# FFN products of a transformer block in scaled fp16 parts, with the raw W1/W3 tile scaled on ScalarE

## The reference

```python
xn = layernorm(x)                               # no gain, no bias
q, k, v = heads(xn @ Wq.T), heads(xn @ Wk.T), heads(xn @ Wv.T)
attn = softmax(causal(q @ k.T / sqrt(32)))
s = merge(attn @ v) @ Wo.T
hidden = silu(xn @ W1.T) * (xn @ W3.T)          # [2, 1024, 2048]
g = silu(fwht(hidden) @ W2.T)                   # Walsh-Hadamard transform over 2048
out = x + s * g
```

## Time and profile before

| | before |
|---|---|
| time, median of 3 runs | 972.14 us (972.06 to 972.33) |
| the profiled execution: its time | 972.55 us |
| the profiled execution: its span | 970.8 us |
| TensorE busy (matmuls) | 959.4 us, 99% |
| VectorE busy | 707.1 us, 73% |
| ScalarE busy | 565.7 us, 58% |
| GpSimd busy | 357.2 us, 37% |
| DMA | 110.58 MB, mean 114 GB/s |

### The profile page before, as it was taken

One profiled execution on the slowest core, in us unless ns is written; L12 is line 12 of the kernel. 1 busy time (PEld: TensorE's weight loads), 2 busy tenths in 40 slices (PEclk: granted clock), 3 DMA queues, 4 the chain that ended last, 5 costly groups with the idle time before them and its releaser, 6 DMA issues. The chain is left out here.

```text
span 970.8 us, 18488 instructions
## 1 busy us (share of the span) xinstructions
PE 959.4 (99%) x6392; PEld 797.7 (82%) x6392; DVE 707.1 (73%) x1441; ACT 565.7 (58%) x1172; POOL 357.2 (37%) x587
## 2 busy tenths in 40 slices
PE   8999999999999999999999999999999999999997
PEld 7888888888888887888888888888888888878886
DVE  7777888888888887755554578888888888833343
ACT  4324777777777786623334166777777777832221
POOL 1896764656656442000001024453443543500000
PEclk9999999999999999999999999999999999999999
DMA  9793235232232405951145523233223232181111
GB/s 285 259 271 110 77 89 142 78 88 56 77 89 56 121 23 201 345 203 44 45 174 204 174 55 88 57 78 89 55 78 88 56 78 56 45 342 49 43 44 44
DMA packets 55757, 110.58 MB, mean 114 GB/s; under 512 B 5360, under 2 KB 22384, under 8 KB 55152
## 3 DMA queue, kind: packets, MB, share of 16 engines
q1 hardware_dynamic: 55664, 109.40, 37.1%
HBM read 75.56 MB, written 33.55 MB: 112 GB/s over the span
## 5 line engine op out<-in xcount | busy, mean ns | idle before, releaser
L1024 DVE TENSOR_TENSOR p_lo<-stage,p_hi 128x512 f16<-128x512 f32 (+2 forms) x288 | 188.3, 654 | 58.4 <-ACT p_hi L743 58.0
L1337 PE MATMUL f<-xt_hi,w_hi 128*128 128x512 f32 x512 | 202.0, 394 | 0.0
L1337 PE MATMUL f<-xt_hi,w_lo 128*128 128x512 f32 x512 | 201.8, 394 | 0.0
L1337 PE MATMUL f<-xt_lo,w_hi 128*128 128x512 f32 x512 | 201.5, 394 | 0.0
L733 ACT ACTIVATE stage<-s 128x512 f32<-128x512 f32 (+2 forms) x288 | 150.8, 524 | 82.9 <-PE s L1298 81.1
L743 ACT ACTIVATE p_hi<-stage 128x512 f16<-128x512 f32 (+2 forms) x288 | 158.8, 551 | 24.9 <-POOL stage L595 20.2
L1298 PE MATMUL s<-qk_st 98*128 98x512 f32 (+2 forms) x384 | 141.4, 369 | 0.0
L1011 DVE CUSTOM_DVE_ANT_0 m<-m,causal 128x1024 f32<-128x1024 f32 (+3 forms) x128 | 131.0, 1023 | 2.7 <-PE m L1282 2.7
L602 POOL TENSOR_TENSOR w_lo<-w,w_hi 128x256 fp32r<-128x256 f32 x128 | 118.3, 953 | 28.5 <-ACT w_hi L764 27.2
L595 POOL TENSOR_SCALAR_AFFINE_SELECT stage<-stage 128x128 f32<-128x128 f32 x192 | 57.4, 306 | 179.0 <-ACT stage L733 178.2
L1337 PEld LDWEIGHTS f<-xt_lo,w_hi 128*128 128x128 f32 x512 | 96.6, 189 | 18.2
(11 more groups left out here) (179 smaller groups left out, 1831.3 us busy)
## 6 DMA issues: line engine op xcount, KB each, us to landing
qk_st<-qk_parts SPq DMA_DIRECT2D x96, 256.0 KB, 4.3
w<-w1w SPq DMA_DIRECT2D x32, 512.0 KB, 3.6
qk_parts<-qk_hi SPq DMA_DIRECT2D x32, 256.0 KB, 3.2
qk_parts<-qk_lo SPq DMA_DIRECT2D x32, 256.0 KB, 4.3
wht_in<-w SPq DMA_DIRECT2D x4, 1024.0 KB, 10.9
w_butterflied<-wht_in SPq DMA_DIRECT2D x4, 1024.0 KB, 5.9
w_transformed<-g_hi SPq DMA_DIRECT2D x8, 512.0 KB, 3.2
w_transformed<-g_lo SPq DMA_DIRECT2D x8, 512.0 KB, 4.7
```

The source lines that it names most:

```text
L1024: dve.tensor_tensor(p_lo[s][:], expd[q % NE][:, 0:end - need], p_hi[s][:], ALU.subtract).then_inc(p_lo_done, 1)
L1337: mm = pe.matmul(F[m][:, 0, :], w, v, start=k == 0, stop=k == GMM - 1)
```

## The change

The FFN's up-projections use fp16 parts in place of fp32r parts, three matmuls for a product as before.

- x: a second pair of transposed tiles, x16_hi and x16_lo, is made from the same PSUM bank, times 2048 (X_TOP): one operation on ScalarE and one on VectorE for each of the 8 tiles of a batch, after the groups in X16_AFTER. A bank is given to the next transpose, to `bound_of_v` and to `transpose_v_scale` only when x16_lo of its tile is done. xt_hi and xt_lo stay, for q, k and v.
- W1/W3: in the first batch each of the 16 tiles gets a power of two from its sum of squares. ScalarE squares the tile (`w13_squares`, with a sum for each partition), TensorE adds over partitions with a matmul of ones in the last columns of bank X (`sum_of_squares`), VectorE makes the power, the scale and the factors that undo it, in five small operations (`scale_of_w13`). This is done for tile 0, for tiles 1 to 3, and for four groups of three. Tile 0 is squared in w13; SP loads tiles 1 to 15 once more for it (`scan_w13`, into stage, wv_raw and a new buffer scan). In heads 0 to 11 the Square stands in slot 5.
- In both batches ScalarE multiplies the raw tile by its scale, in place, in two operations of 128x512 (`scale_w13`) in slot 1, before `w13_high` in slot 2. The first tile of a batch is scaled and split after V tile 1 and no longer after group 8.
- tanh takes its scale from w13_half, and `hide` multiplies by w13_unscale.
- TensorE's order: in a slot with a context one of the slot's FFN matmuls is kept back until behind the context (`kept`).
- Buffers are laid out anew: p_hi and p_lo share their room with xt_hi and xt_lo; x16_hi and x16_lo are new.

The diff, cut to its core (layout, semaphores and the waits for the last columns of bank X are left out):

```diff
@@ -40,6 +40,8 @@
+ONES_AFTER = [3, 4, 5]
+X_TOP = 2048.0
 W2_SCALE = 0.5 * float(HID) ** -0.5
@@ -63,7 +65,7 @@
 COPY_AT = [8, 4]
-W13_AT = 2
+SQUARES_AT, W13_AT = 5, 2
 WO_AT = [1, 2, 7, 9]
@@ -77,6 +79,12 @@
 XT_AFTER = {4: (4,), 5: (5,), 6: (6, 7)}
+X16_AFTER = {2: (0,), 3: (1,), 4: (2, 3), 7: (6, 7), 8: (4,), 9: (5,)}
+X16_ORDER = [t for g in sorted(X16_AFTER) for t in X16_AFTER[g]]
+SCAN_AFTER = {10: (1,), 13: (2, 3)}
+SQUARES_AFTER = {8: (0,), 13: (1,)}
+SQUARES_OF_V = {4: (2,), 5: (3,)}
+SCAN_FIRST, SCAN_GROUP = 4, 3
 SPLIT_WK_AFTER, ROOT_AFTER = 1, 2
@@ -458,6 +517,8 @@
                         load_stack(sp, n + 2)
+                        if b == 0 and j + SCAN_FIRST < NH:
+                            scan_w13(j + SCAN_FIRST)
                         load_w13(n + 2)
@@ -599,7 +660,8 @@
                 at = (slice(None), piece // 2, slice(piece % 2 * (D // 2), (piece % 2 + 1) * (D // 2)))
-                pool.tensor_tensor(w13_lo[n % 2][at], w13[at], w13_hi[n % 2][at].bitcast(F32), ALU.subtract
+                pool.wait_ge(w13_scaled, 2 * n + piece // 2 + 1)
+                pool.tensor_tensor(w13_lo[n % 2][at], w13[at], w13_hi[n % 2][at], ALU.subtract
                                    ).then_inc(w13_lo_done, 1)
@@ -684,6 +747,11 @@
+
+            def x16(b, t):
+                act.wait_ge(xt_lo_done, b * NT + t + 1)
+                act.activation(x16_hi[:, :, t * P:(t + 1) * P], xt_bank(t).rearrange("p (k c) -> p k c", k=KT),
+                               ACT.Copy, scale=X_TOP).then_inc(x16_hi_done, 1)
@@ -712,8 +780,11 @@
                             split_wv(b, kt)
-                    if g == 2 * KT:
-                        w13_high(b * NH)
+                    for t in X16_AFTER.get(g, ()):
+                        x16(b, t)
+                    if b == 0:
+                        for t in SQUARES_AFTER.get(g, ()):
+                            w13_squares(t)
                 if b == 0:
@@ -722,8 +793,23 @@
                                    ACT.Copy).then_inc(proj_hi_done, 1)
+                    if t == 1:
+                        scale_w13(b * NH)
+                        w13_high(b * NH)
+                    if b == 0:
+                        for tile in SQUARES_OF_V.get(t, ()):
+                            w13_squares(tile)
                     if t == MT_BEFORE - 1:
...
+
+            def scale_w13(n):
+
+                act.wait_ge(w13_in, (n + 1) * 16)
+                if n < NH:
+                    act.wait_ge(w13_scale_step, scale_steps(n))
+                for m in range(2):
+                    act.activation(w13[:, m, :], w13[:, m, :], ACT.Copy, scale=w13_scale[:, n % NH:n % NH + 1]
+                                   ).then_inc(w13_scaled, 1)
@@ -755,16 +841,32 @@
                     act.wait_ge(wht_stored, D // P * 16)
-                act.activation(hidden_part(n, c), F[0][:], ACT.Tanh, scale=0.5).then_inc(tanh_done, 1)
+                after(act, w13_scale_step, scale_steps(n) if n < NH else 0)
+                act.activation(hidden_part(n, c), F[0][:], ACT.Tanh, scale=w13_half[:, n % NH:n % NH + 1]).then_inc(tanh_done, 1)
+
+            def w13_squares(n):
+
+                if n == 0:
+                    act.wait_ge(w13_in, 16)
+                else:
+                    act.wait_ge(scan_in[n % 3], (n + 2) // 3 * 16)
+                act.wait_ge(ssq_ready, 1)
+                act.activation(scan_tile(n) if n else w13_hi[0][:], scan_tile(n), ACT.Square,
+                               accum_out=w13_ssq[:, n:n + 1]).then_inc(w13_sum, 1)
...
+                if n < NH:
+                    act.wait_ge(w13_scale_step, scale_steps(n))
                 act.wait_ge(w13_in, (n + 1) * 16)
                 after(act, ffn_ps, (n - 1) * GROUPS)
+                act.wait_ge(w13_scaled, 2 * n + 2)
                 act.activation(w13_hi[n % 2][:], w13[:], ACT.Copy).then_inc(w13_hi_done, 1)
...
                 act.wait_ge(mt_ps, n + 1)
+                if n - 1 in SUM_PLAN:
+                    act.wait_ge(w13_sum_ps, SUM_PLAN[n - 1] + 1)
                 after(act, m_in, n * 32)
@@ -787,6 +889,10 @@
                             tanh(n0 + jf, c)
+                    if b == 0 and s == SQUARES_AT and j + SCAN_FIRST < NH:
+                        w13_squares(j + SCAN_FIRST)
+                    if s == W13_AT - 1 and j + 1 < NH:
+                        scale_w13(n0 + j + 1)
                     if s == W13_AT and j + 1 < NH:
@@ -947,6 +1053,30 @@
+            def x16(b, t):
+                dve.wait_ge(x16_hi_done, x16_no(b, t))
+                at = (slice(None), slice(None), slice(t * P, (t + 1) * P))
+                dve.scalar_tensor_tensor(x16_lo[at], xt_bank(t).rearrange("p (k c) -> p k c", k=KT), X_TOP,
+                                         x16_hi[at], ALU.mult, ALU.subtract).then_inc(x16_lo_done, 1)
+
+            def scale_of_w13(n):
+
+                at = (slice(None), tiles_of(n))
+                power, scale = (v[at].bitcast(mybir.dt.int32) for v in (w13_pow, w13_scale))
+                dve.wait_ge(w13_sum_ps, n + 1)
+                dve.tensor_scalar(power, w13_sum_bank(n).bitcast(mybir.dt.int32), 1, 0x7F800000,
+                                  ALU.logical_shift_right, ALU.bitwise_and).then_inc(w13_scale_step, 1)
+                dve.wait_ge(w13_scale_step, 5 * n + 1)
+                dve.tensor_scalar(scale, power, 0x7F800000, 0, ALU.bitwise_xor, ALU.bitwise_or
+                                  ).then_inc(w13_scale_step, 1)
+                dve.tensor_scalar(w13_half[at], w13_pow[at], 2.0 ** 49 / X_TOP, None, ALU.mult
+                                  ).then_inc(w13_scale_step, 1)
+                dve.scalar_tensor_tensor(w13_unscale[at], w13_pow[at], 2.0 ** 100 / X_TOP ** 2, w13_pow[at], ALU.mult,
+                                         ALU.mult).then_inc(w13_scale_step, 1)
+                dve.wait_ge(w13_scale_step, 5 * n + 2)
+                dve.tensor_scalar(w13_scale[at], w13_scale[at], 2.0 ** -51, 2.0 ** 76, ALU.mult, ALU.min
+                                  ).then_inc(w13_scale_step, 1)
+
@@ -994,10 +1126,15 @@
                                       ALU.subtract).then_inc(proj_lo_done, 1)
-                    if 3 <= t < 6:
-                        dve.memset(k_st[t - 3][STACK:STACK + 2, :].bitcast(F32), 1.0).then_inc(ones_ready, 1)
+                    if b == 0 and t == 0:
+                        scale_of_w13(0)
+                    if t in ONES_AFTER:
+                        dve.memset(k_st[ONES_AFTER.index(t)][STACK:STACK + 2, :].bitcast(F32), 1.0
+                                   ).then_inc(ones_ready, 1)
                     if t == MT_BEFORE - 1:
                         maxima_lo(b * NH)
+                        if b == 0:
+                            scale_of_w13(1)
                 for r in range(FIRST_MAX_AT.count(None)):
@@ -1049,8 +1186,9 @@
                 dve.wait_ge(ffn_ps, n * GROUPS + 2 * c + 2)
-                dve.tensor_tensor(hidden_part(n, c), hidden_part(n, c), F[1][:], ALU.mult
-                                  ).then_inc(hidden_done, 1)
+                after(dve, w13_scale_step, scale_steps(n) if n < NH else 0)
+                dve.scalar_tensor_tensor(hidden_part(n, c), hidden_part(n, c), w13_unscale[:, n % NH:n % NH + 1],
+                                         F[1][:], ALU.mult, ALU.mult).then_inc(hidden_done, 1)
@@ -1167,7 +1307,7 @@
                 if t >= 4:
-                    pe.wait_ge(xt_lo_done, b * NT + t - 3)
+                    pe.wait_ge(x16_lo_done, x16_no(b, t - 4))
                 for kt in range(KT):
@@ -1264,9 +1410,16 @@
                 pe.wait_ge(v_scale_step, 2)
+                pe.wait_ge(x16_lo_done, x16_no(0, 7))
                 for kt in range(KT):
...
+
+            def sum_of_squares(n):
+
+                pe.wait_ge(w13_sum, scan_groups[n][-1] + 1)
+                pe.matmul(w13_sum_bank(n), ones_r[:].bitcast(F32), w13_ssq[:, tiles_of(n)], start=True, stop=True
+                          ).then_inc(w13_sum_ps, 1)
@@ -1333,7 +1490,7 @@
                     w = (w13_hi, w13_hi, w13_lo)[p][n % 2][:, m, kt * P:(kt + 1) * P]
-                    v = (xt_hi, xt_lo, xt_hi)[p][:, kt, c * W:(c + 1) * W]
+                    v = (x16_hi, x16_lo, x16_hi)[p][:, kt, c * W:(c + 1) * W]
                     mm = pe.matmul(F[m][:, 0, :], w, v, start=k == 0, stop=k == GMM - 1)
@@ -1342,16 +1499,21 @@
+
+                def some_ffn(at, upto):
+                    while at < upto:
+                        j, i = divmod(at, GROUPS * GMM)
+                        end = min(GROUPS * GMM, i + upto - at)
+                        ffn(n0 + j, i, end)
+                        at += end - i
+
...
                     at = ffn_upto(g - 1)
-                    while at < ffn_upto(g):
-                        j, i = divmod(at, GROUPS * GMM)
-                        end = min(GROUPS * GMM, i + ffn_upto(g) - at)
-                        ffn(n0 + j, i, end)
-                        at += end - i
```

(7 more changed lines are left out.)

80 lines of the change are left out of this document (67 added, 13 removed).

## The result

The changed kernel takes 976.59 us (median of 20 runs, 973.51 to 981.31) beside 973.03 us for the kernel before (20 runs, 972.06 to 975.03): 1.0037 times the time before, with a 95% interval of 1.0026 to 1.0048. The forecast of 951 us, its range and its sign were wrong. The profiled execution took 981.31 us (span 979.6), the slowest of the 20, so its stalls are larger than those of a median run.

What follows compares the result with a forecast made beforehand. TensorE, busy 99% of the span, was taken as the bound. From 972.55 us: -26.2 heads, +1.8 sums of squares, +2.4 first projection, +0.5 stage ends, together -21.5, gave 951 us; range 945 to 964.

Steps and rivals of the forecast that it cites:

- FFN matmuls of 216 ns: FFN products in fp16: each of 1536 matmuls takes 216 ns, 14 less, gaining 21.5 us, 0.67 a head.
- Changes of type: TensorE's queue in a head: leaving fp16 gains 0.25 us, ten more entries into fp16 cost 0.10 us.
- the exits: fp32r scores behind a context: a kept FFN matmul hides their weight load, gaining 3 x 0.085 = 0.25 us a head.
- the sum: Heads: 18.0 - 0.67 - 0.25 + 0.10 = 17.2 us each, -26.2 us over 32 heads.
- Sums of squares: Six small fp32 matmuls on TensorE in the first batch, 0.3 us each: +1.8 us, bounds 0.2 and 4.
- First projection: x16 tiles delay the fifth transpose by 0.5 us and bound_of_v to 42.5: +2.4 us in all, bounds 0 and 4.
- Square without table loads: ScalarE in heads 0 to 11: a 128x1024 Square was priced at 1.05 us, up to 1.3, without table loads.
- rival (3): Square brings two table loads of 1283 ns each, stopping TensorE in 12 heads: +23, 974 to 980 us; chance 0.06.
- It holds, narrowly, at no cost: First batch's heads: the Square at slot 5 delays exps until slot 10, with 0.3 us left there, costing nothing.
- VectorE 15.9 of 17.2, still below TensorE: VectorE in a head keeps its operations, busy 15.9 of 17.2 us, so TensorE stays slowest.
- Rival (1): ScalarE or VectorE becomes slowest in the first batch; twelve Square heads stay at 18.0: 961, up to 964 us; chance 0.11.
- The loads find the DMA engines 28% used: Scan loads, 15 x 512 KB behind load_stack in SP's queue, meet DMA engines 28% used in a head.

Runs made afterwards that it cites:

- e6: Changed kernel with tile 8's scan load early, Square at slot 4, Squares of tiles 4 to 15 on 8 columns and head butterflies on 8 elements: 959.44 us.
- e10: Kernel before plus one 128x1024 ScalarE Square at slot 5 of heads 0 to 9 of the first batch, with no load: 981.68 us, 1.0092.
- e13: e10 with GpSimd's butterflies in the heads on 8 elements, against the kernel before: 972.61 us, 0.9995.
- e14: Changed kernel with Squares at slot 9 instead of 5 and tiles 4 to 15 in groups of two instead of three: 964.72 us, 0.9922.
- e12: Changed kernel with tile 8's scan early, Square at slot 4, store_slab(2) in head 2, butterflies after the masks of slot 1 and before slot 8's: 967.69 us.
- e1: Changed kernel with the scan load of tile 8 issued ahead of the slab store and load in SP's queue: 973.32 us, 1.0001.

## Why the prediction was wrong, step by step

**FFN matmuls of 216 ns: right.** In the second batch's heads fp16 FFN matmuls that follow one another start 216 ns apart (median), the fp32r ones 233 before. The mean of the page's row fell from 394 to 382 ns.

**Changes of type: the exits were mis-sized.** A head in the middle of the second batch went from 18.02 to 17.31 us (mean of 13), 0.71 less where the sum had 0.82. An entry costs what I took: the second FFN matmul behind a score starts 227 ns after the first instead of 216. The exits don't give 0.25. Behind two of a head's three contexts, 0.08 us is gained as forecast. Behind the third stands the short transpose, which is fp32 too, and it meets the exposed load in the score's place: from the last context matmul to the FFN matmul behind the score it was 29, 28 and 316 ns, and is 99, 110, 28 and 421, which is 0.07 us more after the 216 of the kept matmul.

```profile
666.74 0.19 PE L1475 MATMUL o<-vparts,p_lo 128*128 128x65 f16 x1
666.83 0.27 PE L1445 MATMUL xs<-ident,mx 128*8 128x128 f32 x1
666.94 0.38 PE L1494 MATMUL f<-x_hi,w_hi 128*128 128x512 f16 x1
666.97 0.58 PE L1455 MATMUL s<-qk_st 98*128 98x512 f32 x1
667.39 0.39 PE L1494 MATMUL f<-x_lo,w_hi 128*128 128x512 f16 x1
```

So the exits give 0.09 us a head. The heads of the second batch gained 9.9 us, and twice that is some 6 us short of the 26.2 of the sum, of which the sums of squares below give 1 back; e6, with its 956 to 959, shows it beside 951. It was a mis-sized term, no more.

**Sums of squares: mis-sized, harmlessly.** Each takes about 0.14 us (start to start 26 to 31 and 112 ns for its two passes), 0.8 us for six instead of 1.8.

**First projection: the waits are right, the total in part luck.** +2.6 us for +2.4, with `bound_of_v` waiting for x16_lo:

```profile
42.46 0.70 PE L1408 MATMUL m<-w_lo,ones_r 128*128 128x512 f32 x2 [1.34 <-DVE x_lo L1059]
```

It stood at 40.10. This wait and the one of the fifth transpose (0.5, as forecast) make 1.8 us; a pause of 0.97 us ahead of a group's matmul at 38.14, which waits for nothing that the profile shows, is in no term of the sum (0.4 before). Over the twelve kernels with x16 the first score is 1.1 to 3.6 us later than 87.5.

**Square without table loads: right.** 1.06 us and 0.19 for reading the sum, with no load around it; rival (3) is out. The same tanh before and after, with the scale as a constant and from a tile:

```profile
L758 ACT ACTIVATE hidden<-f 128x512 f32<-128x512 f32 x64 | 37.7, 589 | 0.0
```

```profile
L845 ACT ACTIVATE hidden<-f,w_half 128x512 f32<-128x512 f32 x64 | 43.6, 682 | 0.0
```

The operand from a tile costs 93 ns, and I had taken 0.1. The Trainium skill, "ScalarE: Activation LUTs", section "What ACT_TABLE_LOAD costs", gives 93 ns for a pointer operand, and the trace agrees. ScalarE was busy 15.35 and 14.40 us in the two heads shown, where I had 16.1 and 14.9, so its share of a head wasn't what failed.

**"It holds, narrowly, at no cost": this step failed.** I followed the Square through ScalarE's queue and the two score banks, and stopped there. The delay doesn't end at the score. It passes from exp to p_hi and from p_hi to p_lo, and there it moves a VectorE operation onto a GpSimd operation; that makes `hide` late, and TensorE waits for `hide` in slot 1, up to 1.02 us a head and 9.0 us in all. In slot 10, which I had as the tightest place with 0.3 us left, 0.3 us is lost as well: not at the score, but behind VectorE's m_lo, which waits for ScalarE's m_hi. e10 and e13 show it without the rest of the change: 9 us for ten Squares, and nothing when the butterflies are small.

**"VectorE 15.9 of 17.2, still below TensorE": failed too.** I took VectorE's 15.86 us as a sum of operations with fixed lengths. They aren't: the head of the earlier trace rows holds one p_lo of 1.27 us that needs 0.56 alone, and in a shorter head the second butterfly meets a p_lo as well. In e14 and e12 it is busy 17.25 and 17.56 us in the heads shown, as much as TensorE's new 17.3. In the changed kernel's own head it is 16.81 of 18.70, less than the two collisions alone would add to 15.44, as p_lo of slots 4 and 5 meet less of GpSimd's w13_lo pieces there (0.72 and 0.74 us; 0.99 and 1.18 in the second batch): there VectorE isn't full, it is late where TensorE needs it. Rival (1) named the right engines but priced them as if a head could at worst stay at 18.0.

**"The loads find the DMA engines 28% used": failed in one place.** That share is from a head at 201 us. Around 163 us SP issues the slab and the stack ahead of the scan, and the scan is issued 6.9 us into the head. This cost 7.6 us in the profiled execution. The times also spread, 973.5 to 981.3 us over 20 runs where the kernel before spreads over 3, but e1, in which no Square waits for its load, spreads over 9 us in 10 runs: what spreads them stays open.

**The account.** Of 25.6 us between 951.0 and 976.6, e6 shows 5 to 8 that were never to be had (956 without the slab's head, 959 with it); the other 17 to 21 are the Square with the butterflies, and the late scan. The profiled execution, 4.7 us above the median, agrees roughly: 12.7 lost in the first batch's heads where 9.9 should have been gained, 22.6 in all.

## What to carry to other kernels

When an engine's delay is followed through a schedule, follow it to the last engine of the chain, and look at what each delayed operation will then run beside; the length of a VectorE operation with two SBUF operands is only valid for what GpSimd did at that moment. And look at where TensorE waits before calling an engine full: e12 moved the loss from one slot to another at 94 to 98% busy. A resource with slack in a head of 18.0 us has to be looked at again at the length that is forecast. An average DMA share says nothing of the one place where a queue holds a big transfer: look there first for a new load that a compute queue will wait for.

## What the runs showed of the hardware

- VectorE's tensor_tensor with both inputs in SBUF makes little headway beside a tensor_tensor of GpSimd that started first. In e10 the p_lo of 384 columns starts 0.42 us after a butterfly and has 0.86 us of it ahead; with its own 0.56 (e13) that makes 1.42, and it took 1.28. GpSimd's own length stays at 1.27 to 1.29. Where the p_lo starts first, it is the butterfly that gets longer, as in the kernel before:

```profile
231.33 0.41 DVE L1024 TENSOR_TENSOR p_lo<-stage,p_hi 128x256 f16<-128x256 f32 x1
231.40 1.50 POOL L581 TENSOR_TENSOR wht_in<-wht_in 128x512 f32<-128x512 f32 x1
```

  The Trainium skill, "SBUF — State Buffer", section "Who interferes with whom", says that a VectorE instruction with two SBUF inputs contends with a GpSimd instruction that reads SBUF, and its section "SBUF: two separate sides" that whichever starts first has the shared pair for the whole instruction. By that the p_lo of 256 columns, which starts with the other butterfly, would take 1.29 + 0.43 = 1.72 us, an estimate; it took 1.56. So the trace agrees, to within 0.16.
- The fp16 w13_lo pieces of GpSimd take 777 ns on average where the fp32r ones took 953; I had allowed for 30% more.
- Not foreseen either: one late load stopped TensorE for 6.25 us and cost it the clock as well, 1.00 before and 0.50 behind.
